# Three edits in a four-layer cross-attention kernel: order of weight splits and loads in layer 2, place of the value-bias work in layer 2, place of the second context sum in layer 3

## Chip, cores and metric

The kernel runs on one core of one Trainium2 chip. The metric is device time in microseconds (us) of one execution, lower is better. The engines are TensorE (PE; its weight loads are PEld), VectorE (DVE), ScalarE (ACT), GpSimd (POOL) and SyncE (SP), which here only issues DMAs.

## What is computed

Eight sequences of 100 tokens of 512 features pass through four layers; each sequence has a context of 361 rows. Layer 0 is a Perceiver-style attention with an MLP, layer 1 an RWKV block. The change is in layers 2 and 3. Layer 2 has two cross-attentions (numbered 1 and 2) of 16 heads of 128 features, and then an MLP; layer 3 has one cross-attention with 32 query heads and 8 key and value heads of 16 features. Cut to what matters:

```python
def _cross_attention(q_in, kv_in, wq, bq, wk, bk, wv, bv, wo, bo, bias_k, bias_v):   # layer 2, twice
    qh = (q_in @ wq + bq).reshape(b, q_len, H, K)
    kh = (kv_in @ wk + bk).reshape(b, t, H, K)
    vh = (kv_in @ wv + bv).reshape(b, t, H, K)
    kh = jnp.concatenate([kh, jnp.broadcast_to(bias_k, (b, 1, H, K))], axis=1)
    vh = jnp.concatenate([vh, jnp.broadcast_to(bias_v, (b, 1, H, K))], axis=1)
    weights = jax.nn.softmax(jnp.einsum('bqhk,bthk->bhqt', qh, kh) / scale, axis=-1)
    return jnp.einsum('bhqt,bthk->bqhk', weights, vh).reshape(b, q_len, H * K) @ wo + bo
```

## The kernel before, in words

The whole program is one launch. Each stage is a block in which the five engines run instruction lists of their own, in order, and wait for each other through semaphores; a block ends when all engines are through with it. Nothing is ordered by a planner: the order of every engine's list is written out by hand. Large fp32 products are made of three reduced-precision ones: a value is rounded to a high half (ACT) and the rest is the low half (DVE or POOL), and `product` (L71, L72, L73) multiplies high by high, high by low and low by high.

**Layer 2** (`layer2_attention`) works in four steps, `half` 0 to 3: two cross-attentions by two groups of four sequences (400 tokens). One SBUF arena (`l2_arena`) holds nearly all its buffers. A half has three phases.

- The **query phase** goes over 16 heads. For each head PE turns the key weight (`turn_keys`, L2385), makes the query (`query`, L71 to L73) and multiplies it by the turned key weight (`turn_queries`, L71 to L73 again), so that scores can be taken against the raw context. ACT rounds the weights and the query (L2607, L2616, L2621); DVE makes the low halves (`split_q_w` L2844, `split_k_w` L2849, `split_queries` L2854). In halves 0 and 2 POOL multiplies the query weight of each head by the key bias (L2345, with L2339 once per pair of heads) into one buffer, `product0`, and DVE adds it up (`reduce_w0`, L2866) before it goes on to the next head's splits. Weights of q and k come in pairs of heads (`load_qk`, L2009), two pairs of buffers.
- The **attention phase** goes over the four sequences. Their context is loaded by POOL (`load_context`, L2300 to L2309: two memsets, five DMAs), two buffers.
- The **value phase** goes again over 16 heads. For head h PE does 12 matmuls (`values`), one for the bias row (`bias_values`, L2493) and then 12 of head h-1 (`project`). ACT rounds the value weight (L2719), the four parts of `u` (L2741), the output weight (L2728) and the result (L2747); POOL makes the low half of the value weight (`split_v_w`, L2322) and of the output weight (L2372); DVE makes the low half of the result (L2943) and of `u` (L2937, four a head). DVE also does the statistics of the next half (`sum_next` L2952 at head 2, `shift_next` at head 3), and POOL the power of minus one half that they need (`invert_next`, L2327, at head 4). POOL's order from the start is: low halves of value weights 0 and 1, then for each head h first that of value weight h (from head 2 on), and then that of output weight h. SP loads value weights in pairs of heads (`load_v`, L2203) into two buffers; pair p is asked for at head 2p, before the output weight of that head (`load_o`, L2209), the bias rows (L2218) and the first column of the probabilities (L2225, L2226).

The **value bias** of both cross-attentions is prepared once, in half 0, before the first head: SP loads it (L2234, L2235) behind the first key biases (L2195, L2196), DVE takes a difference (L2987), ACT rounds it (L2757), DVE takes the rest (L2990), and SP stores six rows to DRAM (L2240) and waits for them. DVE and ACT wait for these in their lists ahead of the splits of head 0, and POOL's list begins with `load_context(0)`, which waits for the stores (`v_stored`), because the context buffer lies over the arena's value-bias rows.

**Layer 3** has a query block (`layer3_queries`) and an attention block (`layer3_attention`). The context of a sequence comes from DRAM as two halves (`load_context`, L3124) into one pair of buffers, and POOL adds them (`sum_context`, L3131) into one of two buffers `cT`, from which PE makes keys (L3152) and values (L3161) for the next sequence. POOL also spreads the queries (`spread_queries`, L3141, 12 instructions a sequence). In the attention block PE does scores (L3484), turns the probabilities (L3492) and sums (L3507, L3510) for 32 heads of each of 8 sequences; DVE stacks the low halves of the next keys (`stack_lo`, L3187) at heads 20, 22, 24 and 26. The sum of sequence 0 is done in the query block; the load and the sum of sequence 1 come at the start of the attention block, and on POOL behind the spreading of the last two pairs of sequence 0.

## Time and profile before

| | us |
|---|---|
| three timed runs, median | 3300.31 |
| three timed runs, lowest and highest | 3297.93, 3303.03 |
| the profiled execution, its own time | 3297.78 |
| its span in the profile | 3296.0 |
| mean granted TensorE clock, share of full speed | 0.962 |

The span is what the engines' records cover; 1.8 us of the profiled execution lie around it. Layer 2's attention lies between about 1110 and 2720 us of the span, layer 3 from about 2900 us to the end. In the rows further down, each line of a timeline gives start, duration, engine, line, operation, output and inputs; the bracket behind it gives how long the engine stood idle before it, and what it is taken to have waited for. "issue" there means that the profile shows no releaser. Where an instruction waits for several semaphores, the profile names the one that came last by its records, which isn't always the right one.

### The profile page before, as it was taken

The numbers are of one execution on the slowest core, as the hardware profiler recorded it, in microseconds if no ns is written. First come the engines' busy times: TensorE is split into PE (matmuls) and PEld (weight loads), VectorE is DVE, ScalarE is ACT, GpSimd is POOL, SyncE is SP. The second block draws the span as 40 slices with busy tenths as digits, with TensorE's granted clock in tenths as the row PEclk, the third lists the DMA queues.
The fourth block names the chain that finished last, engine by engine and source line by source line (L and its number), as shares of the span: only waits on it lengthen the run. The fifth ranks groups of instructions, "written<-read, shape, count | busy, mean of one in ns | idle before, by whom it ended". The sixth has DMA issues, their size and how long they took to land. (4 is left out here: it accounts for less than half of the span.)

```text
span 3296.0 us, 48341 instructions
## 1 busy us (share of the span) xinstructions
PE 3017.6 (92%) x17461; PEld 2573.6 (78%) x17461; DVE 1925.4 (58%) x3925; ACT 1498.1 (45%) x3444; POOL 893.7 (27%) x927
## 2 busy tenths in 40 slices
PE   5999989798878799999999999999999997989997
PEld 4777589484534599989999899998999996965663
DVE  2454442538953476666666776657666565137775
ACT  2544442331111254456544655446554464236773
POOL 0222310326641321133011441104101151046563
PEclk9999989899988899999999999999999997988999
DMA  4231020100001320114101241103301023021110
GB/s 127 68 99 44 27 77 1 37 27 15 0 0 39 92 92 28 43 61 129 59 28 47 81 143 45 47 28 95 120 28 55 20 85 105 1 78 40 41 43 21
DMA packets 132159, 182.79 MB, mean 55 GB/s; under 512 B 17839, under 2 KB 99740, under 8 KB 131932
## 3 DMA queue, kind: packets, MB, share of 16 engines
q1 hardware_dynamic: 119204, 143.96, 14.1%
q0 software_dynamic: 12544, 35.77, 3.5%
q8 instruction: 140, 2.29, 0.3%
q14 instruction: 87, 0.71, 0.1%
q10 hardware_dynamic: 184, 0.05, 0.0%
HBM read 165.88 MB, written 13.86 MB: 55 GB/s over the span
## 5 line engine op out<-in xcount | busy, mean ns | idle before, releaser
L71 PE MATMUL l2a<-l_arena,l_arena 128*128 128x400 f32 (+2 forms) x1856 | 642.5, 346 | 36.2 <-issue 15.8
L72 PE MATMUL l2a<-l_arena,l_arena 128*128 128x400 f32 (+2 forms) x1856 | 629.9, 339 | 0.0
L73 PE MATMUL l2a<-l_arena,l_arena 128*128 128x400 f32 (+2 forms) x1856 | 629.5, 339 | 0.0
L71 PEld LDWEIGHTS l2a<-l_arena,l_arena 128*128 128x128 f32 (+1 forms) x1856 | 349.5, 188 | 48.6 <-issue 35.5
L72 PEld LDWEIGHTS l2a<-l_arena,l_arena 128*128 128x128 f32 (+1 forms) x1856 | 350.7, 189 | 2.6
L73 PEld LDWEIGHTS l2a<-l_arena,l_arena 128*128 128x128 f32 (+1 forms) x1856 | 350.0, 189 | 2.0
L2694 ACT ACTIVATE l_arena<-l2a 121x384 fp32r<-121x384 f32 (+1 forms) x208 | 99.5, 479 | 438.3 <-PE l2a L2447 438.3
L2467 PE MATMUL l2a<-l_arena,l_arena 121*128 121x384 f32 (+1 forms) x768 | 279.6, 364 | 0.0
L2468 PE MATMUL l2a<-l_arena,l_arena 121*128 121x384 f32 (+1 forms) x768 | 263.8, 344 | 0.0
L2469 PE MATMUL l2a<-l_arena,l_arena 121*128 121x384 f32 (+1 forms) x768 | 263.8, 344 | 0.0
L2317 POOL DMA_DIRECT2D p_dram_layer<-l_arena x128 | 62.9, 497 | 653.0 <-DVE l_arena L2912 651.3
L2890 DVE TENSOR_REDUCE l_arena<-l2a 128x1 f32<-128x362 f32 (+1 forms) x208 | 110.9, 533 | 203.3 <-PE l2a L73 199.4
L3546 ACT ACTIVATE probs<-probs,neg_max 100x363 f32<-100x363 f32 x256 | 151.5, 595 | 100.4 <-DVE neg_max L3608 97.0
L2937 DVE TENSOR_TENSOR l_arena<-Qp_layer,l_arena 128x400 fp32r<-128x400 f32 x256 | 164.0, 699 | 36.2 <-ACT l_arena L2741 36.1
L3608 DVE CUSTOM_DVE_ANT_0 probs<-scores,mask 100x363 f32<-100x363 f32 x256 | 134.1, 532 | 84.5 <-PE scores L3484 78.9
L432 POOL TENSOR_SCALAR probs<-probs,inverse 100x464 f32<-100x464 f32 x128 | 83.5, 653 | 299.3 <-DVE inverse L636 299.1
L3492 PEld LDWEIGHTS turned<-ident,probs 100*121 100x121 f32 x768 | 122.3, 199 | 40.5 <-ACT probs L3546 21.7
L2468 PEld LDWEIGHTS l2a<-l_arena,l_arena 121*128 121x128 f32 x768 | 144.9, 189 | 2.3
L2469 PEld LDWEIGHTS l2a<-l_arena,l_arena 121*128 121x128 f32 x768 | 144.1, 188 | 3.0
L2467 PEld LDWEIGHTS l2a<-l_arena,l_arena 121*128 121x128 f32 x768 | 144.4, 188 | 2.4
L3492 PE MATMUL turned<-ident,probs 100*121 100x100 f32 x768 | 130.3, 281 | 17.2 <-ACT probs L3546 11.2
L2912 DVE TENSOR_TENSOR l_arena<-l2a,l_arena 121x384 fp32r<-121x384 f32 (+1 forms) x208 | 112.8, 542 | 53.3 <-ACT l_arena L2694 53.3
(444 smaller groups left out, 7016.9 us busy)
## 6 DMA issues: line engine op xcount, KB each, us to landing
l_arena<-in_L_xattn_wq_dram SPq DMA_DIRECT2D x32, 512.0 KB, 3.5
l_arena<-in_L_xattn_wk_dram SPq DMA_DIRECT2D x32, 512.0 KB, 4.7
l_arena<-in_L_xattn_wv_dram SPq DMA_DIRECT2D x32, 512.0 KB, 3.5
l_arena<-in_L_xattn_wo_dram SPq DMA_DIRECT2D x64, 256.0 KB, 2.7
l_arena<-ctxT_hi POOLq DMA_DIRECT2D x16, 724.0 KB, 4.5
l_arena<-ctxT_lo POOLq DMA_DIRECT2D x16, 724.0 KB, 6.1
l0mlp_staged<-in_L_xattn_mlp_w_dram SPq DMA_DIRECT2D x16, 512.0 KB, 4.1
l2mlp_staged<-in_L_xattn_w_fc_dram SPq DMA_DIRECT2D x16, 512.0 KB, 4.3
```

What stands on the lines that cost most here:

```text
L71: pe.matmul(out, cut_a(a.hi), cut_b(b.hi), start=start, stop=False)
L72: pe.matmul(out, cut_a(a.hi), cut_b(b.lo), start=False, stop=False)
L73: return pe.matmul(out, cut_a(a.lo), cut_b(b.hi), start=False, stop=stop)
L2467: pe.matmul(out, c_hi[s][0:T2, n, rows], probsT.hi[0:T2, n, ring], start=(n == 0), stop=False)
L2468: pe.matmul(out, c_hi[s][0:T2, n, rows], probsT.lo[0:T2, n, ring], start=False, stop=False)
L2469: mm = pe.matmul(out, c_lo[s][0:T2, n, rows], probsT.hi[0:T2, n, ring], start=False, stop=(n == NT2 - 1))
L2890: dve.tensor_reduce(neg_max[0:rows, i:i + 1], ps_s[i % 3][0:rows, 1:1 + KEYS2], AX.X, ALU.max, negate=True).then_inc(maxed, 1)
L2912: dve.tensor_tensor(probsT.lo[0:T2, :, cols], ps_t[i % 2][0:T2, 0:NT2 * P].rearrange("p (n l) -> p n l", l=P)[:, :, 0:n], probsT.hi[0:T2, ...
L2937: dve.tensor_tensor(u[h % 2].lo[:, t, :].rearrange("p (b q) -> p b q", q=L), head_columns(Qp, h)[:, t], u[h % 2].hi[:, t, :].bitcast(F32). ...
L3492: mm = pe.transpose(ps_turned[h % 2][0:T3, j * L:(j + 1) * L], probs[h % PROBS][:, j * T3:(j + 1) * T3], k.ident[0:L, 0:L])
L3546: act.activation(probs[h % PROBS][:], probs[h % PROBS][:], ACT.Exp, bias=neg_max[:, h % H3:h % H3 + 1], scale=-1.0).then_inc(exped, 1)
L3608: dve.tensor_tensor_reduce(probs[h % PROBS][:], ps_scores[h % SCORES][0:L, 0:N3], mask_add[b % 2][:], -1.0, 3e38, ALU.add, ALU.min, neg_ma ...
```

## The change

Layer 2, value phase. SP asks for the value weights of pair 2 right behind those of pairs 0 and 1, and for pair p (from 3 on) at the end of head 2p-3's steps. POOL makes the low half of value weight h+2 behind that of output weight h.

Layer 2, half 0. SP loads the value bias ahead of the first key biases. DVE takes the difference at head 1 and the rest at head 3, ACT rounds at head 2. SP stores the rows behind the loads of pair 2 of the query and key weights, without waiting; it waits for them only before the first use in the value phase. POOL loads context 0 at head 6 instead of ahead of head 0, and the wait for the stores there is gone.

Layer 3. SP loads the context of sequence 1 in the query block, as soon as sum 0 is done, and POOL adds it there, ahead of the query spreading. In the attention block, for sequences from 2 on, POOL waits before the sum also for all low halves of the last keys (`lo_stacked`).

```diff
@@ layer2_attention, SP
             for half in range(STEPS):
-                load_kb(half, 0)
-                load_kb(half, 1)
                 if half == 0:
                     for n, layer in enumerate((1, 2)):
                         sp.dma_start(v_rows[0:H2, n, 0, :], bias_v).then_inc(v_loaded, 16)
                         sp.dma_start(v_rows[0:H2, n, 1, :], ins[f"L2_xattn_bv{layer}"].rearrange("(h d) -> h d", d=DH2)
                                      ).then_inc(v_loaded, 16)
-                    sp.wait_ge(v_split, 1)
...
-                    sp.wait_ge(v_stored, 96)
+                load_kb(half, 0)
+                load_kb(half, 1)
                 for p in range(2, H2 // 2):
                     load_qk(half, p)
                     load_kb(half, p)
+                    if half == 0 and p == 2:
+                        sp.wait_ge(v_split, 1)
+                        for row, part in enumerate((v_hi, v_hi, v_lo)):
+                            for n in range(LAYERS2):
+                                sp.dma_start(vb_dram[n, row].rearrange("(h d) -> h d", d=DH2),
+                                             part[0:H2, n, :].bitcast(F32)).then_inc(v_stored, 16)
...
                 load_v(half, 1)
                 load_o(half, 1)
+                load_v(half, 2)
                 wait_p0(half + 1)
+                if half == 0:
+                    sp.wait_ge(v_stored, 96)
...
                 for h in range(2, H2):
-                    if h % 2 == 0 and h >= 4:
-                        load_v(half, h // 2)
                     load_o(half, h)
                     load_vb(half, h)
                     load_p0(half, h)
+                    if h % 2 == 1 and 3 <= (h + 3) // 2 < H2 // 2:
+                        load_v(half, (h + 3) // 2)
@@ layer2_attention, POOL
-                load_context(QUAD * half)
+                if half:
+                    load_context(QUAD * half)
                 for h in range(H2):
+                    if half == 0 and h == 6:
+                        load_context(0)
...
-                    if h >= 2:
-                        split_v_w(half, h)
                     if h == 4 and half + 1 < STEPS:
                         invert_next(half)
                     pool.wait_ge(o_w_hi, H + 1)
                     pool.tensor_tensor(Wo[h % 2].lo, staged_o[h % 2], Wo[h % 2].hi.bitcast(F32), ALU.subtract
                                        ).then_inc(o_w_lo, 1)
+                    if h + 2 < H2:
+                        split_v_w(half, h + 2)
@@ layer2_attention, ACT
-            act.wait_ge(v_diff, 1)
-            act.activation(v_hi[0:H2], v_rows[0:H2, :, 2, :], ACT.Copy).then_inc(v_rounded, 1)
...
+                    if half == 0 and h == 2:
+                        act.wait_ge(v_diff, 1)
+                        act.activation(v_hi[0:H2], v_rows[0:H2, :, 2, :], ACT.Copy).then_inc(v_rounded, 1)
@@ layer2_attention, DVE
-            dve.wait_ge(v_loaded, 64)
...
                 for h in range(H2):
+                    if half == 0 and h == 1:
+                        dve.wait_ge(v_loaded, 64)
+                        dve.tensor_tensor(v_rows[0:H2, :, 2, :], v_rows[0:H2, :, 0, :], v_rows[0:H2, :, 1, :], ALU.subtract
+                                          ).then_inc(v_diff, 1)
+                    if half == 0 and h == 3:
+                        dve.wait_ge(v_rounded, 1)
+                        dve.tensor_tensor(v_lo[0:H2], v_rows[0:H2, :, 2, :], v_hi[0:H2].bitcast(F32), ALU.subtract
+                                          ).then_inc(v_split, 1)
@@ layer3_queries
             batch.load_mask(sp, ins, 0)
+            sp.wait_ge(batch.cT_summed, 1)
+            batch.load_context(sp, k, 1)
...
             batch.sum_context(pool, 0)
             pool.wait_ge(batch.rows_ready, 1)
+            batch.sum_context(pool, 1)
@@ layer3_attention
             for b in range(1, B):
-                sp.wait_ge(batch.cT_summed, b)
-                batch.load_context(sp, k, b)
                 if b >= 2:
+                    sp.wait_ge(batch.cT_summed, b)
+                    batch.load_context(sp, k, b)
                     sp.wait_ge(shifted, H3 * (b - 1))
...
             for b in range(1, B):
+                pool.wait_ge(headed, BLOCKS * PAIRS * b)
                 if b >= 2:
                     pool.wait_ge(batch.values_done, b - 1)
-                pool.wait_ge(headed, BLOCKS * PAIRS * b)
-                batch.sum_context(pool, b)
-                if b >= 2:
+                    pool.wait_ge(batch.lo_stacked, PAIRS * b)
+                    batch.sum_context(pool, b)
                     pool.wait_ge(scored, H3 * (b - 1))
```

## Rows read from the trace of the kernel before

**Rows 1.** The page's first part: busy time, share of the span and instructions
```profile
PE 3017.6 (92%) x17461; PEld 2573.6 (78%) x17461; DVE 1925.4 (58%) x3925; ACT 1498.1 (45%) x3444; POOL 893.7 (27%) x927
```

**Rows 2.** Waits of PE, whole span: us in total, times, longest
```profile
PE l2a L71 <- issue: 15.8, 11, 2.0
```

**Rows 3.** Timeline of PE, first heads of layer 2's half 0
```profile
1123.56 0.67 PE L71 MATMUL l2a<-l_arena,l_arena 128*128 128x400 f32 x1 [3.97 <-DVE l_arena L2844]
...
1134.63 0.42 PE L71 MATMUL l2a<-l_arena,l_arena 128*128 128x400 f32 x1 [3.56 <-DVE l_arena L2844]
...
1140.62 0.60 PE L2385 MATMUL l2a<-ident,l_arena 128*128 128x128 f32 x4
...
1145.42 0.60 PE L2385 MATMUL l2a<-ident,l_arena 128*128 128x128 f32 x4
```

**Rows 4.** Timeline of DVE in the same stretch
```profile
1120.75 0.41 DVE L2987 TENSOR_TENSOR l_arena<-l_arena 16x256 f32<-16x256 f32 x1 [5.86 <-DMA l_arena<-in_L_xattn_bv_dram]
...
1131.84 0.69 DVE L2866 TENSOR_REDUCE W_layer<-l_arena 128x4 f32<-128x512 f32 x1 [7.89 <-POOL l_arena L2345]
```

**Rows 5.** Timeline of POOL in half 0's query phase
```profile
1125.79 0.52 POOL L2300 MEMSET l_arena<- 1x512 f32 x1 [13.61 <-DMA vb_layer<-l_arena]
...
1130.54 1.27 POOL L2345 TENSOR_TENSOR l_arena<-l_arena,l_arena 128x512 f32<-128x512 f32 x1
```

**Rows 6.** Windows: us, busy of PE, PEld, DVE, ACT, POOL; clock; DMA; GB/s
```profile
1123.56:1131.07 7.51, 7.51 (x28) 7.18 (x28) 0.39 (x1) 2.12 (x4) 5.18 (x9) 0.64 0.41 131
```

**Rows 7.** View of line L2196, the key-bias loads: issue to landing
```profile
DMA to landing us min/median/max: 4.0/5.0/6.0
```

**Rows 8.** Timeline of SP's queue: the six stores of the value bias
```profile
1122.09 2.63 SPq L2240 DMA_DIRECT2D vb_layer<-l_arena  x6
```

**Rows 9.** Timeline of PE, value phase of half 1
```profile
1845.33 0.34 PE L2493 MATMUL l2a<-l_arena,vb_layer 128*128 128x400 f32 x1
...
1849.88 0.42 PE L71 MATMUL l2a<-l_arena,l_arena 128*128 128x400 f32 x1 [1.99 <-issue]
...
1911.84 0.35 PE L2493 MATMUL l2a<-l_arena,vb_layer 128*128 128x400 f32 x1
...
1916.41 0.34 PE L2493 MATMUL l2a<-l_arena,vb_layer 128*128 128x400 f32 x1
```

**Rows 10.** Timeline of DVE, first heads of that value phase
```profile
1845.38 2.03 DVE L2937 TENSOR_TENSOR l_arena<-Qp_layer,l_arena 128x400 fp32r<-128x400 f32 x4 [0.38 <-ACT l_arena L2741]
...
1848.53 5.34 DVE L2937 TENSOR_TENSOR l_arena<-Qp_layer,l_arena 128x400 fp32r<-128x400 f32 x4 [0.31 <-ACT l_arena L2741]
1853.79 0.62 DVE L2943 SCALAR_TENSOR_TENSOR l_arena<-l2a,params,l_arena 128x400 fp32r<-128x400 f32 x1
...
1856.69 2.47 DVE L2952 BATCH_NORM_STATS2 l_arena<-X 100x6 f32<-100x512 f32 x4
```

**Rows 11.** Timeline of POOL there: low half of value weight 2
```profile
1848.52 1.26 POOL L2322 TENSOR_TENSOR l_arena<-l_arena,l_arena 128x512 fp32r<-128x512 f32 x1
```

**Rows 12.** Timeline of PE, layer 3, first sequence
```profile
2953.63 1.58 PE L3152 MATMUL work<-cT,Wk 128*128 128x363 f32 x2 [4.03 <-POOL cT L3131]
...
2978.36 0.53 PE L3492 MATMUL turned<-ident,probs 100*121 100x100 f32 x3 [2.00 <-DVE probsT L3615]
```

**Rows 13.** Timeline of DVE there: low half of a key stack
```profile
2974.13 3.12 DVE L3187 TENSOR_TENSOR keys<-keysT,keys_hi 32x363 fp32r<-32x363 f32 x1
```

**Rows 14.** Windows again, early attention block of layer 3
```profile
2980.00:2990.00 10.00, 10.00 (x48) 7.54 (x48) 6.29 (x23) 7.07 (x15) 7.86 (x6) 0.50 0.50 163
```

**Rows 15.** Timeline of POOL, layer 3
```profile
2940.48 0.11 POOL L3424 MEMSET ones<- 121x16 f32 x1 [7.26 <-POOLq L3207]
...
2981.75 3.10 POOL L3141 TENSOR_TENSOR q_heads<-queries_hi,head_rows 32x800 fp32r<-32x800 f32 x2 [4.89 <-PE scores L3484]
...
3024.04 3.10 POOL L3141 TENSOR_TENSOR q_heads<-queries_hi,head_rows 32x800 fp32r<-32x800 f32 x2 [19.89 <-PE scores L3484]
...
3060.99 3.10 POOL L3141 TENSOR_TENSOR q_heads<-queries_hi,head_rows 32x800 fp32r<-32x800 f32 x2 [14.55 <-PE scores L3484]
```

More of the change, by code:

```diff
@@ L2236, in _ @@
                                      ).then_inc(v_loaded, 16)
-                    sp.wait_ge(v_split, 1)
-                    for row, part in enumerate((v_hi, v_hi, v_lo)):
-                        for n in range(LAYERS2):
-                            sp.dma_start(vb_dram[n, row].rearrange("(h d) -> h d", d=DH2), part[0:H2, n, :].bitcast(F32)
-                                         ).then_inc(v_stored, 16)
-                    sp.wait_ge(v_stored, 96)
+                load_kb(half, 0)
+                load_kb(half, 1)
                 for p in range(2, H2 // 2):
@@ L2985, in _ @@
             split_q_w(0, 0)
-            dve.wait_ge(v_loaded, 64)
-            dve.tensor_tensor(v_rows[0:H2, :, 2, :], v_rows[0:H2, :, 0, :], v_rows[0:H2, :, 1, :], ALU.subtract
-                              ).then_inc(v_diff, 1)
-            dve.wait_ge(v_rounded, 1)
-            dve.tensor_tensor(v_lo[0:H2], v_rows[0:H2, :, 2, :], v_hi[0:H2].bitcast(F32), ALU.subtract).then_inc(v_split, 1)
             for half in range(STEPS):
```

## The prediction, on record before the changed kernel was run

> **What bounds the kernel now.** I read the busy shares first: TensorE (PE) is busy in 92% of the span and no other engine in more than 58% [rows 1]. So an edit pays by what it takes out of PE's stalls, and by what PE loses to a low clock after a stall; work of DVE, ACT, POOL and SP costs nothing while PE doesn't wait for it. The waits of PE come second. A group stands out whose releaser the profile doesn't know: L71 behind "issue", 15.8 us in 11 waits of at most 2.0 [rows 2]. Then the timelines of the engines, side by side, at each stall.
>
> **Start of half 0.** PE stands 3.97 us at 1123.56 and 3.56 us at 1134.63, both times for L2844, the low half of a query weight [rows 3]. DVE shows why. Ahead of the splits of head 0 it waited 5.86 us for the DMA of the value bias, and later 7.89 us for POOL's first product [rows 4]. POOL stood 13.61 us until 1125.79, because `load_context(0)` waits for the stores of the value bias; only behind its memsets and five DMAs comes the product, at 1130.54 [rows 5]. This is one chain: load, difference, rounding, rest, six stores, context, product, sum, split. The clock fell with it: granted 0.64 between 1123.56 and 1131.07 [rows 6].
>
> **Value phases.** Each head is 25 matmuls, and where nothing disturbs it its period is 4.57 us (1911.84 to 1916.41) [rows 9]. From the bias matmul of head 1 to that of head 15 half 1 takes 71.08 us. Fourteen periods are 64.0, and four heads in which PE also turns a weight of the next half add an estimated 0.35 each: 65.4. So 5.7 us are lost in this half. At head 2 the cause is visible: PE goes on at 1849.88 [rows 9], 0.10 after the low half of value weight 2 is through (1848.52 + 1.26) [rows 11], which stands on POOL behind the output weight of head 1.
>
> **Layer 3.** PE waits 4.03 us for the sum of context 1, and 2.00 at 2978.36 for DVE [rows 12], which had spent 3.12 us on a low half of keys [rows 13]. Then the clock is at 0.50, the lower level, for ten us [rows 14].
>
> **The change, part by part.** The sum is made against the profiled execution's own time, 3297.8, which is 2.5 us under the median of the runs, at their low end; the same differences are then set on the median, 3300.3.
>
> A. Value bias out of the way. DVE's 5.86 and POOL's 13.61 go, so both PE stalls go: 3.97 + 3.56 = 7.5. The clock: from 1123.56 to 1131.07 (1134.63 less its 3.56) PE takes 7.51 us for what takes 4.80 later, 2.7 lost; the 5.99 from 1134.63 to 1140.62 I set against an estimated 4.2 at full clock, 1.8 lost [rows 3, 6]. In all 12.0. What is late next: the key bias now lies behind four loads on SP and lands about 5.0 us after its issue [rows 7], then product (1.27), sum (0.69) and the splits of head 2 follow [rows 4, 5]; I get them ready within 0.2 us of PE. The two DVE operations now stand at heads 1 and 3, 0.41 each [rows 4]; one of them may show, 0.4. The stores take SP's queue for 2.63 [rows 8], so pair 3 of the weights comes some 3 us later; their cover is the pair ahead of them, two periods of 4.80, and without it 3 us would be lost once. SP's later wait for the stores, ahead of the bias rows, is for DMAs hundreds of us old: nothing. The context at head 6: two memsets at 0.52 and five DMA issues take POOL about 4 us (1125.79 to 1130.54 is 4.75 [rows 5]), against two products of 1.27 in a period of 4.80: product 7 may be late by 1 to 2 us, and DVE and ACT work about a head ahead of PE, so 0; without that cover 2. The transfers of the context meet those of the weights of pair 4, which I expect hidden as well. **A gives 11.4**, bounds 7 (the first stall back in part and the context seen) and 12.
>
> B. Value weights early. POOL makes the low half of weight h+2 behind output weight h, more than a head ahead of PE, and SP loads the pairs a head sooner. At most all of 4 x 5.7 = 22.8 goes. What stays: DVE's four parts of `u` take 2.03 alone, and took 5.34 at head 2 while POOL made weights beside them [rows 10]. POOL's two operations a head don't go away, they only come in another order. With the durations of half 1, I have left: about 1.0 at head 2 (the parts of `u` late), 1.5 at head 3, where the statistics (2.47 [rows 10]) delay the low half of the result, 0.5 at head 4 for POOL's power; 3 in each of halves 0 to 2, and 1 in half 3, which has no next statistics. 22.8 - 10 = 12.8. **B gives 13**, bounds 3 (only the wait at head 2, about 2 in two halves of the four) and 22.8. SP has more room for `load_o`, since pair 2 is asked for before the wait for the probabilities; the wait for a free buffer in `load_v` is for a low half that is now made earlier: nothing.
> Here a rule must be weighed. The row shows 5.34 - 2.03 = 3.3 us more, the length of 2.6 of POOL's 1.26 [rows 10, 11]. The Trainium skill (SBUF — State Buffer, Who interferes with whom) says that a DVE instruction with two SBUF inputs contends with a GpSimd instruction that reads SBUF, and that whoever issued first holds the shared ports for the whole instruction while the other blocks. By it B could be a loss, the third rival below; the trace agrees in size, but the steady heads at 4.57 with the same two POOL operations speak against a loss each head.
>
> C. Layer 3. The sum of context 1 moves into the query block, where POOL stood idle 7.26 us before the next block [rows 15]. With the wait for its load it delays the spreading there by about 1 us, hidden behind PE's queries; if that cover is gone, 1 us. The stall of 4.03 goes. The wait for `lo_stacked` keeps later sums off DVE's low halves; behind it on POOL stands the spreading, which waits for `scored` anyway, 19.89 and 14.55 us in later sequences [rows 15]: nothing. In sequence 0 no sum is left there, so 3.12 should fall towards the half of it or less, and the 2.00 goes. The clock: the period from 2981.75 to 3024.04 is 42.3 us, the next one 36.95 [rows 15], 5.3 lost with a clock of 0.50 [rows 14]. Without the stalls in front it may still fall; I take two thirds, 3.5. **C gives 9.5**, bounds 3 (a stall is left, clock low) and 4.0 + 2.0 + 5.3 = 11.3.
>
> Sum: 11.4 + 13 + 9.5 = 33.9. On the profiled execution 3263.9, on the median **3266.4**. With the parts erring independently this case spans some 3257 to 3275.
>
> **The rivals.**
> 1. Less than forecast: the lag of DVE in the value phases eats most of B (5 left), and layer 3's second sequence stays at the low clock (C 6). For it: 5.34, and a clock that fell to 0.50 long after the stall of 4.03. 11.4 + 5 + 6 = 22: about 3278. Chance 0.18.
> 2. More: PE never waits in the value phases and the clock holds. 12 + 22.8 + 11.3 = 46: about 3254. Against it: the statistics keep their place. 0.12.
> 3. The shared access as an exclusive lock in every head: 2.03 + 0.62 + 2 x 1.26 = 5.17 a head for DVE, 0.60 over 4.57, in 56 periods 34, less the 22.8 lost now: 11 slower in B, so 33.9 - 13 - 11 = 10 gained in all, about 3290. The rule of the Trainium skill quoted above would make this of it. 0.03.
> 4. Slower, DVE the bound of the value phases: if the new order puts POOL beside the parts of `u` in each head, they take 5.34, with the split of the result 0.62, 5.96 a head [rows 10]. That is 1.39 over 4.57, 78 in 56 periods, less 22.8: 55 lost against 21 won in A and C, about 3334. It turns slower where a head's DVE chain passes about 5.4. Against: 2.03 + 0.62 leaves 1.9 us a head, and one POOL operation needs 1.26. 0.04.
> 5. No change: each stall only changes its name (pair 3 late in A, `u` in B, `probsT` in C), or the loads aren't early because a buffer is still held. Gain under 6.6, about 3298. The three stalls have different causes, so hardly all. 0.03.
>
> **Numbers.** Forecast 0.60, the rivals 0.18, 0.12, 0.03, 0.04, 0.03. 0.2% is 6.6 us, about what a measurement of this kernel can tell from no change. Faster by more: 0.60 + 0.18 + 0.12 + 0.03 = 0.93; within: 0.03; slower: 0.04. The range 3250 to 3284 takes in cases one and two and the bounds of the terms, and leaves out rivals 3 to 5 and the tails.
>
> **What would show it.** Right: PE's stalls of 3.97 and 3.56 gone, the turn of 1140.62 some 11 us earlier; the granted clock there well over 0.64. In the value phases L71 behind "issue" under about 5 us, POOL's L2322 more than a head ahead of PE, 71.08 down to about 68. In layer 3 no wait for L3131, L3187 well under 3.12, the first `scored` period near 37. Wrong: L2937 slower in most heads and PE behind L2943 or L2741 (rivals 1, 3, 4); a new wait at heads 6 to 8 of half 0 for a split or a load; PE or POOL waiting in the query block of layer 3; a period of 42 with the stalls gone.

## The result, and the profile after

The changed kernel takes 3278.41 us (median of 5 runs, 3273.79 to 3284.71), the kernel before 3300.83 in the same comparison. The ratio is 0.9937, with a 95% interval of 0.9920 to 0.9955: 22.4 us faster by the medians. The forecast was 3266.4, which is 33.9 us faster. The profiled execution has a span of 3277.1 us against 3296.0.

The two spans, cut at the same instructions of PE, tell where the 18.9 us went. Each figure is a difference of two start times in PE's timeline.

| stretch, us | before | after | |
|---|---|---|---|
| up to layer 2's first matmul (no edit there) | 1111.30 | 1109.36 | -1.94 |
| half 0, from there to the first bias matmul | 335.23 | 331.55 | -3.68 |
| the same of halves 1 to 3 (from the last bias matmul of the half before) | 971.41 | 970.94 | -0.47 |
| value phases, first to last bias matmul, halves 0, 1, 2, 3 | 74.26, 73.46, 75.97, 70.51 | 75.73, 75.99, 75.14, 67.69 | +0.35 |
| to layer 3's first query matmul | 196.02 | 195.88 | -0.14 |
| layer 3, query block from there | 32.62 | 31.15 | -1.47 |
| layer 3, from the first score to the end | 355.22 | 343.67 | -11.55 |

So the forecast's three parts came out as 3.7 instead of 11.4 (A, the start of half 0), -0.35 instead of 13 (B, the value phases), and 13.0 instead of 9.5 (C, layer 3). Of C's 13.0 the 1.47 of the query block is not the edit's: eleven profiled executions have the second sum in that block, and in nine of them it takes 32.20 to 32.72 us, as it does before (32.62); only two have 31.15 and 31.06. That leaves 11.55. A further 2.6 of the 18.9 lie in stretches without an edit of their own.

The page's first part, which answers to [rows 1]; PE's share is the same, and DVE is 62 us busier with the same 3925 instructions:

```profile
PE 3010.9 (92%) x17461; PEld 2569.7 (78%) x17461; DVE 1987.4 (61%) x3925; ACT 1495.7 (46%) x3444; POOL 897.0 (27%) x927
```

Waits of PE in the changed kernel (us in total, times, longest; lines for other waits are left out), which answer to [rows 2]. Line numbers have moved: the splits of `u` are L2944 (L2937 before), of the result L2950 (L2943), of a query weight L2851 (L2844):

```profile
PE l2a L71 <- DVE l_arena L2944: 13.0, 13, 3.0
...
PE l2a L71 <- DVE l_arena L2851: 6.7, 3, 3.5
...
PE l2a L71 <- DVE l_arena L2950: 5.0, 3, 1.7
...
PE l2a L2391 <- DMA l_arena<-in_L_xattn_wk_dram: 4.7, 1, 4.7
```

The 15.8 us behind "issue" are gone, as forecast. In their place stand 13.0 for L2944 (2.2 before), and a new wait of 4.7 for the DMA of a key weight.

**Start of half 0.** Both stalls of [rows 3] are gone. But the turn of the key weight of head 8 (the first of pair 4), which began at 1155.76, waited, and so did the query behind it. In PE's timeline:

```profile
1155.76 1.11 PE L2391 MATMUL l2a<-ident,l_arena 128*128 128x128 f32 x4 [4.69 <-DMA l_arena<-in_L_xattn_wk_dram]
1157.64 0.67 PE L71 MATMUL l2a<-l_arena,l_arena 128*128 128x400 f32 x1 [0.77 <-DVE l_arena L2851]
```

The timeline of SP has the issue of that weight, the one of POOL the context of sequence 0 right behind it:

```profile
1140.26 1.20 SPq L2009 DMA_DIRECT2D l_arena<-in_L_xattn_wk_dram  x1
```

```profile
1140.62 0.80 POOL L2306 DMA_DIRECT2D l_arena<-ctxT_hi  x1
1141.43 0.54 POOL L2306 DMA_DIRECT2D l_arena<-ctxT_lo  x1
1141.96 1.63 POOL L2312 DMA_DIRECT2D l_arena<-in_ctx_dram  x3
```

The weight landed 15.5 us after its issue, where the key weights of pairs 2 and 3 took 4.55 and 4.75. The DMA queues show why. While the context's transfers ran (1143 to 1152), queue q0 moved 2.06 MB, nearly all of the context, and q1, which has SP's loads (this weight, and behind it the next pair), only 0.61, some 70 GB/s. From 1154 to 1157, with the context nearly through, q1 moved 0.96 MB in 3 us, some 320 GB/s (columns: packets, MB, share of 16 engines):

```profile
q0 software_dynamic: 471, 2.06, 74.4%
q1 hardware_dynamic: 616, 0.61, 27.2%
```

```profile
q1 hardware_dynamic: 984, 0.96, 105.6%
```

Behind the wait the clock was at 0.57 (windows, with the columns of [rows 6]):

```profile
1155.76:1162.00 6.24, 5.47 (x19) 5.06 (x20) 5.18 (x7) 3.20 (x7) 2.00 (x2) 0.57 0.30 96
1162.00:1172.00 10.00, 10.00 (x61) 9.93 (x60) 8.65 (x13) 5.73 (x12) 3.73 (x3) 1.00 0.38 125
```

**Value phases.** PE, half 1; 1840.19 and 1913.80 are the bias matmuls of heads 1 and 15, so the 71.08 of [rows 9] became 73.61:

```profile
1840.19 0.34 PE L2499 MATMUL l2a<-l_arena,vb_layer 128*128 128x400 f32 x1
...
1857.28 0.42 PE L71 MATMUL l2a<-l_arena,l_arena 128*128 128x400 f32 x1 [1.66 <-DVE l_arena L2950]
...
1867.48 0.50 PE L71 MATMUL l2a<-l_arena,l_arena 128*128 128x400 f32 x1 [3.04 <-DVE l_arena L2944]
...
1913.80 0.34 PE L2499 MATMUL l2a<-l_arena,vb_layer 128*128 128x400 f32 x1
```

POOL in the same stretch:

```profile
1859.64 1.04 POOL L2330 TENSOR_TENSOR l_arena<-l_arena,minus_half 100x4 f32<-100x4 f32 x1 [5.86 <-DVE l_arena L2968]
1860.67 1.28 POOL L2376 TENSOR_TENSOR l_arena<-l_arena,l_arena 128x512 fp32r<-128x512 f32 x1
...
1865.65 1.25 POOL L2376 TENSOR_TENSOR l_arena<-l_arena,l_arena 128x512 fp32r<-128x512 f32 x1
```

DVE, which answers to [rows 10]:

```profile
1840.23 5.20 DVE L2944 TENSOR_TENSOR l_arena<-Qp_layer,l_arena 128x400 fp32r<-128x400 f32 x4 [0.38 <-ACT l_arena L2747]
...
1854.14 2.46 DVE L2959 BATCH_NORM_STATS2 l_arena<-X 100x6 f32<-100x512 f32 x4
...
1860.01 8.78 DVE L2944 TENSOR_TENSOR l_arena<-Qp_layer,l_arena 128x400 fp32r<-128x400 f32 x4
```

Read them together. POOL stands 5.86 us at the power (L2330), which waits for DVE's statistics, and the low halves behind it wait too. Then it runs five of them in a row, from 1860.67 to 1866.90. Beside them DVE's four parts of `u` need 8.78 us, and PE waits 3.04. Behind that wait PE's clock is at 0.69 for 5.5 us, so this period of 9.56 is 5.0 over the undisturbed 4.57 and not only 3.04:

```profile
1867.48:1873.00 5.52, 5.52 (x22) 5.48 (x23) 4.43 (x9) 1.33 (x3) 0.14 (x1) 0.69 0.64 217
```

In half 3, where there are no statistics and no power, PE never waits after head 2 and each period is 4.57. But look at DVE there:

```profile
2682.98 4.10 DVE L2944 TENSOR_TENSOR l_arena<-Qp_layer,l_arena 128x400 fp32r<-128x400 f32 x4
2687.01 0.62 DVE L2950 SCALAR_TENSOR_TENSOR l_arena<-l2a,params,l_arena 128x400 fp32r<-128x400 f32 x1
2687.55 4.10 DVE L2944 TENSOR_TENSOR l_arena<-Qp_layer,l_arena 128x400 fp32r<-128x400 f32 x4
```

The four parts take 4.10 where they take 2.03 alone, with no idle time of DVE around them. Half 3 still runs at PE's pace, but DVE has nothing left.

**Layer 3.** The wait for L3131 and the 2.00 of [rows 12] are gone, the low half that took 3.12 [rows 13] takes 0.53, and the clock of the second sequence is 1.00 (windows of the first and the second sequence):

```profile
2933.43:2970.13 36.70, 34.55 (x205) 25.07 (x206) 28.75 (x94) 28.15 (x60) 34.26 (x21) 0.82 0.17 52
2970.13:3007.05 36.92, 34.01 (x257) 22.14 (x257) 28.78 (x99) 27.93 (x59) 21.40 (x13) 1.00 0.14 47
```

### The profile page after: what moved, and what is told of

Same layout as the page of the kernel before. It is cut to its first block and busy times, and to the rows that moved or that the text cites. A ratio compares the mean times of both kernels' runs of the same rounds, so it can differ in the third digit from the quotient of the medians.

```text
span 3277.1 us, 48347 instructions
## 1 busy us (share of the span) xinstructions
PE 3010.9 (92%) x17461; PEld 2569.7 (78%) x17461; DVE 1987.4 (61%) x3925; ACT 1495.7 (46%) x3444; POOL 897.0 (27%) x927
## 3 DMA queue, kind: packets, MB, share of 16 engines
q8 instruction: 140, 2.29, 0.3%
## 5 line engine op out<-in xcount | busy, mean ns | idle before, releaser
L2944 DVE TENSOR_TENSOR l_arena<-Qp_layer,l_arena 128x400 fp32r<-128x400 f32 x256 | 243.8, 1008 | 10.3 <-ACT l_arena L2747 9.9
L583 ACT ACTIVATE probs<-probs,neg_max 100x464 f32<-100x464 f32 x128 | 87.1, 681 | 122.5 <-DVE neg_max L669 121.7
```

The lines of the kernel that those rows point to most:

```text
L2944: dve.tensor_tensor(u[h % 2].lo[:, t, :].rearrange("p (b q) -> p b q", q=L), head_columns(Qp, h)[:, t], u[h % 2].hi[:, t, :].bitcast(F32). ...
```

## The experiments

Twelve kernels, each timed four to seven times beside the kernel before. Ratios are to the kernel before of the same comparison (medians 3299.61, 3300.36 and 3302.31), with 95% intervals. Phase lengths are from each one's profiled execution, cut as in the table above.

### Context in pieces

```diff
                     if half == 0 and h == 6:
                         load_context(0)
+                    if half == 0 and h in (8, 10, 12, 14):
+                        load_piece(0, h // 2 - 3)
```

`load_context(0)` keeps the two memsets and the first DMA, and each `load_piece` issues one of the other four.

> The changed kernel, with the five DMAs of context 0 issued at heads 6, 8, 10, 12 and 14 instead of all at head 6. Theory: in the changed kernel PE's wait of 4.69 us for a key weight at 1155.76 (and 0.77 behind it, and a half clock after it) comes from the context's transfers, which share the DMA engines with pair 4 of the weights. Then the 4.69 goes, no other wait above 1 us comes in this phase, and the kernel takes 5 to 8 us less than the changed one: 3271 to 3273. Rival: pair 4 is late because the six stores held SP's queue for 2.64 us. Then the wait stays at 4 us or more and the time stays at 3278.

Measured: 3275.15 (3269.36 to 3277.00), ratio 0.9923 (0.9910 to 0.9936). The wait for the key weight is gone, and half 0 takes 322.74 us up to its first bias matmul instead of 331.55. The mechanism is as expected; the gain in the median, 3 us, is under the 5 to 8 expected, and the intervals of the two ratios overlap. The other runs say why. Nine profiled executions have the context in one go at head 6, the changed kernel's and those of eight variants below. PE's wait in them was 4.96, 4.69, 3.76, 3.62, 2.29 and 0.75 us, and in three there was none; half 0 took 331.89 us in the worst and 322.74 in the best. The four with pieces all lie between 322.55 and 322.87. So the collision comes in some executions and not in others, and costs up to 9 us where it comes. The six stores hold SP's queue in all of them alike, so they alone don't cause it.

Could the four without a wait be luck, as the three of the nine are? The issue of that key weight on SP tells the cases apart. It took 0.82 to 1.57 us in the six executions with a wait, and the weight landed 11.5 to 15.7 us after it; in the three without, it took 0.51 to 0.70, and the weight landed after 4.8 to 5.9. With pieces it was long in two of the four as well (1.43 and 1.58), but the weight then landed after 8.8 and 8.3 us, within the 10.8 after which PE is ready for it. This is the issue in the run with pieces:

```profile
1141.80 1.43 SPq L2009 DMA_DIRECT2D l_arena<-in_L_xattn_wk_dram  x1
```

So the pieces don't avoid the meeting, they make it short enough to hide. What makes SP's issue long in one execution and not in the next was not tried.

### The power later

```diff
-                    if h == 4 and half + 1 < STEPS:
+                    if h == 6 and half + 1 < STEPS:
                         invert_next(half)
```

> The changed kernel, with POOL's power (next inverse) at head 6 of the value phase instead of head 4. Theory: at head 4 POOL waits 5.9 us for the statistics and holds five low halves back, which then run as one burst of 6.2 us; DVE's four parts of u (8.78 us at 1860.01) can't proceed beside it, and PE waits 3.04 at 1867.48. Without the hold the burst goes: the period of 9.56 (8.42, 8.72 in the other halves) at head 5 falls to 5 or 6, some 3.5 us less in each of halves 0 to 2, in all 10 us less: 3268. The wait of 1.66 for the low half of the result at head 4 stays. Rival: the parts of u are slow wherever POOL works beside them, with or without a hold; then the lost time spreads over heads 5 to 8 and the kernel takes less than 3 us less.

Measured: 3260.19 (3259.20 to 3262.16), ratio 0.9881 (0.9867 to 0.9895). The value phases are 71.01, 71.02, 71.01 and 67.67, which is 13.8 us less in sum than in the changed kernel, and the period at head 5 is 4.56 where 5 or 6 was expected. The time is 18 us under the changed kernel's, 8 more than expected; about 4 of these 18 lie outside the value phases and were not traced. The 1.66 at head 4 stays. POOL no longer stands before the power, in half 1:

```profile
1857.65 1.54 POOL L2325 TENSOR_TENSOR l_arena<-l_arena,l_arena 128x512 fp32r<-128x512 f32 x1 [1.51 <-ACT l_arena L2725]
1859.16 1.38 POOL L2330 TENSOR_TENSOR l_arena<-l_arena,minus_half 100x4 f32<-100x4 f32 x1
1860.52 1.28 POOL L2376 TENSOR_TENSOR l_arena<-l_arena,l_arena 128x512 fp32r<-128x512 f32 x1
```

Half of the rival is true: the parts of `u` are slow beside POOL here too (4.22 us at 1858.50 in half 1, 4.10 a head in half 3). Its conclusion falls: no lost time spreads over the heads behind. What costs PE is the burst, not the slowing as such.

### The statistics early

```diff
@@ DVE, end of the attention phase
                     if i == STEPS2:
                         split_u(half, 0, range(2, KT))
+                        if half + 1 < STEPS:
+                            sum_next(half)
+                            shift_next(half)
@@ DVE, value phase
-                        if h == 2:
-                            sum_next(half)
-                        if h == 3:
-                            shift_next(half)
```

> The changed kernel, with the statistics of the next half (sum and shift) moved on DVE from heads 2 and 3 to the end of the attention phase, where DVE stood idle for 4.6 us; POOL's power keeps its place at head 4. Theory: both waits of PE go, the 1.66 (the low half of the result behind 2.47 us of statistics) and the burst behind the power, since what POOL waits for is then long there. The phases of halves 0 to 2 fall from 73.3 to 66 or 67 us: 18 to 21 us less in all, 3257 to 3260. Rival: the lag of DVE comes from the order of POOL's weights alone; then the 1.66 goes but a wait for u at head 5 or 6 stays, and the gain is 5 us.

Measured: 3263.93 (3259.85 to 3265.29), ratio 0.9895 (0.9880 to 0.9909). The value phases are 69.41, 69.42, 69.41 and 67.69 us: 18.6 less in sum, as expected, and PE's waits of 1.66 and 3.04 are both gone. The time is 4 us above the range expected. The phases hold; what the median lacks was not traced to one place. The collision of half 0, absent in this profile, can come in its other executions, and its layer 3 took 347.87 us in this execution where the changed kernel's took 343.67.

### Without B

```diff
@@ SP
                 load_o(half, 1)
-                load_v(half, 2)
...
                 for h in range(2, H2):
+                    if h % 2 == 0 and h >= 4:
+                        load_v(half, h // 2)
...
-                    if h % 2 == 1 and 3 <= (h + 3) // 2 < H2 // 2:
-                        load_v(half, (h + 3) // 2)
@@ POOL
                     H = H2 * half + h
+                    if h >= 2:
+                        split_v_w(half, h)
...
-                    if h + 2 < H2:
-                        split_v_w(half, h + 2)
```

> The changed kernel with the value phases as before: loads of value weights and POOL's order undone, the parts in half 0's start and in layer 3 kept. Theory: by the value phases' own lengths the second part of the change gives nothing (73.35, 73.61, 72.75 and 65.31 us against 71.89, 71.08, 73.59 and 68.13 before, 0.3 longer in sum), so this kernel is within 3 us of the changed one, 3275 to 3281. Rival, the forecast: the part is worth 13 us, and this kernel takes 3291.

Measured: 3276.76 (3272.69 to 3284.16), ratio 0.9932 (0.9919 to 0.9945) against 0.9937. B is worth nothing in the changed kernel. The forecast's 13 us are refuted.

### B's loads alone

Of the diff just above, POOL's part alone.

> The changed kernel with POOL's order in the value phases as before (low half of value weight h ahead of output weight h); SP's early loads stay. Theory: what the second part gains and loses both come from POOL's order. The first bias periods are as before (6.8 at head 1, 6.55 at head 4), no period is over 7, and the phases are 70 to 74 us long; the odd losses of half 3 (periods of 4.8 to 5.1 in every second head) come from late loads and go, so that half 3 is near 69. The kernel is within 3 us of the changed one. Rival: the early loads alone give most of what can be had and the phases of halves 0 to 2 fall to 71 or less.

Measured: 3267.65 (3263.30 to 3273.84), ratio 0.9903 (0.9887 to 0.9918): some 11 us faster than the changed kernel. The value phases are 72.98, 71.95, 72.83 and 68.56, 8.2 less in sum. The periods at head 1 of halves 0 and 2 are 8.00 and 7.84, where none over 7 was expected. Half 3 came out as expected, since its odd losses came from the late loads, but the conclusion that was put first is wrong: B isn't two sides of POOL's order. Its loads gain (9.8 us of phase length against the kernel without B), and its order takes 8.2 of that back. DVE in half 3 of this kernel, and POOL beside it:

```profile
2659.11 2.03 DVE L2944 TENSOR_TENSOR l_arena<-Qp_layer,l_arena 128x400 fp32r<-128x400 f32 x4 [0.31 <-ACT l_arena L2747]
```

```profile
2660.96 1.34 POOL L2378 TENSOR_TENSOR l_arena<-l_arena,l_arena 128x512 fp32r<-128x512 f32 x1 [1.97 <-ACT l_arena L2734]
2662.26 1.29 POOL L2325 TENSOR_TENSOR l_arena<-l_arena,l_arena 128x512 fp32r<-128x512 f32 x1
```

With the old order POOL makes both low halves in a row, nearly all of it behind the four parts, which end at 2661.14. They take 2.03, and DVE has 1.9 us idle in each head. With the new order the same four take 4.10.

### B's order alone

Of the same diff, SP's part alone.

> The changed kernel with SP's loads of value weights as before (pair p asked for at head 2p); POOL's new order stays. Theory: POOL can make a low half two heads ahead only if the weight is there; with the late load ACT rounds it late, POOL waits for it at every even head with the output weight of the next head behind that wait, and PE waits at every second head: half 3 is longer than 67.7, by 1 us at each of six heads, some 73, and the kernel takes 5 to 15 us more than the changed one. Rival: the loads land in time anyway; then half 3 stays at 67.7 and the time is the same.

Measured: 3281.27 (3273.94 to 3285.80), ratio 0.9931 (0.9916 to 0.9946): the same as the changed kernel. Half 3 is 71.08 us (periods up to 6.45) against 67.69, so the late loads cost 3.4 us there, where 5 or 6 were expected. Halves 0 to 2 are 75.34, 73.63 and 75.25, and the whole is not the 5 to 15 us slower that was expected.

### C's sum back

```diff
@@ layer3_queries
-            sp.wait_ge(batch.cT_summed, 1)
-            batch.load_context(sp, k, 1)
...
-            batch.sum_context(pool, 1)
@@ layer3_attention
             for b in range(1, B):
+                sp.wait_ge(batch.cT_summed, b)
+                batch.load_context(sp, k, b)
                 if b >= 2:
-                    sp.wait_ge(batch.cT_summed, b)
-                    batch.load_context(sp, k, b)
...
                     pool.wait_ge(batch.lo_stacked, PAIRS * b)
-                    batch.sum_context(pool, b)
+                batch.sum_context(pool, b)
+                if b >= 2:
                     pool.wait_ge(scored, H3 * (b - 1))
```

> The changed kernel, with the load and the sum of context 1 back at the start of the attention block of layer 3; the wait for the low halves (lo_stacked) of the later sequences stays. Theory: the query-phase sum is worth what the chain there shows, the stall of 4.03 us and the low clock behind it. Then PE waits about 4 us for the sum again, the first sequence and the one behind it are 8 to 12 us longer in sum, and the kernel takes 3286 to 3290 against 3278. Rival: the clock would have fallen anyway and is no part of it; then only 4 us come back, 3282.

Measured: 3281.16 (3276.16 to 3290.32), ratio 0.9949 (0.9931 to 0.9966). The wait for the sum is back in PE's timeline:

```profile
2939.25 1.58 PE L3162 MATMUL work<-cT,Wk 128*128 128x363 f32 x2 [4.04 <-POOL cT L3141]
```

The wait for `probsT` and the low clock in the second sequence (0.95 here) are not. The first sequence takes 38.54 us, against 34.55 in the changed kernel: the 4.0 of the wait. The time is the rival's, but not its reason: the clock didn't fall far, with the stall or without. The time alone doesn't tell the two kernels apart, as their intervals overlap; the timeline does.

### C without the wait for the low halves

```diff
-                    pool.wait_ge(batch.lo_stacked, PAIRS * b)
```

> The changed kernel without POOL's wait for lo_stacked ahead of the sums of layer 3. Theory: the wait keeps the sum of context 2 (3.27 us) off DVE's last low half of keys in the first sequence. Without it that low half takes over 2.5 us again (now 0.53), PE waits 1 to 2 us for the probabilities there, and the clock of the second sequence may fall (up to 5 us): 3279 to 3285. Rival: without the sum of context 1 in the first sequence POOL comes to this sum at another time anyway, and the wait is worth nothing: 3278, with a longest low half under 2 us.

Measured: 3281.11 (3277.19 to 3282.48), ratio 0.9939 (0.9919 to 0.9959). The longest low half is 1.76 us, PE has no wait of 2 us for `probsT`, and the clock of the second sequence is 1.00. The time also lies in the range expected, but the mechanism is the rival's: by the ratios (0.9939 and 0.9937) the wait alone is worth nothing. It is close, though: the last low half of keys began 0.97 us before POOL's sum.

### Without C

Both diffs above together, so that layer 3 is as before.

> The changed kernel with layer 3 as before: sum of context 1 in the attention block, no wait for lo_stacked. Undoing either half of this part alone brought no wait of 2.00 us and no fall of the clock in the second sequence. Theory: the long low half (3.12 us) needs both, a POOL that is a sum late and no wait in front of it; with both undone it is back, PE waits about 2.0 us for probsT near the end of the first sequence, the clock of the second sequence falls to 0.8 or 0.9, and layer 3's attention block is 353 to 357 us long against 343.7 in the changed kernel; the kernel takes 3288 to 3292. Rival: the fall of the clock in the kernel before was chance; then the block is 348 long, as with the sum alone back, and the kernel takes 3282.

Measured: 3292.56 (3287.79 to 3295.76), ratio 0.9972 (0.9959 to 0.9984): 0.35% or 12 us slower than the changed kernel by the ratios, 14 by the medians. The attention block is 357.97 us long, just over the 353 to 357 expected. PE, DVE and POOL near the end of the first sequence:

```profile
2971.67 0.53 PE L3502 MATMUL turned<-ident,probs 100*121 100x100 f32 x3 [2.43 <-DVE probsT L3625]
```

```profile
2967.02 3.54 DVE L3197 TENSOR_TENSOR keys<-keysT,keys_hi 32x363 fp32r<-32x363 f32 x1
```

```profile
2966.92 3.25 POOL L3141 TENSOR_TENSOR cT<-cT_hi,cT_lo 128x1444 f32<-128x1444 f32 x1
```

DVE's instruction begins 0.10 us behind POOL's and ends 0.39 behind it: it did its own half microsecond of work when POOL was through. The clock of the second sequence is 0.77. The kernel before has the same pair, 3.12 us beside a sum that began 0.52 before it. So the dip is no chance; it needs both, a POOL that is a sum late and no wait in front of the next one. Either half of C prevents it, and the parts' gains don't add.

### Both mends together, and a third

The first version has the diffs of "Context in pieces" and "The statistics early". The second has besides:

```diff
-                if half:
+                if half % HALVES:
                     load_context(QUAD * half)
-                    if half == 0 and h == 6:
-                        load_context(0)
-                    if half == 0 and h in (8, 10, 12, 14):
-                        load_piece(0, h // 2 - 3)
+                    if half % HALVES == 0 and h == 6:
+                        load_context(QUAD * half)
+                    if half % HALVES == 0 and h in (8, 10, 12, 14):
+                        load_piece(QUAD * half, h // 2 - 3)
```

> The changed kernel with both mends together: context 0 issued in five pieces at heads 6 to 14, and the statistics of the next half at the end of the attention phase. Theory: the two are in different phases and add up. The mended value phases are 5.7 to 6.6 us shorter each in halves 0 to 2 (69.4 us against 75.1 to 76.0), and half 0's query phase is 322.7 us in every execution, where the changed kernel has 331.6 in some: 3256 to 3260. The spread of its times is smaller than that of the changed kernel's (11 us). Rival: the collision with the weights comes back with pieces at other heads; then its lowest and highest stay 8 us apart and the median is at 3263, as with the statistics alone.

> As the version with both mends, and in half 2 too the context (sequence 8 in the count of both attentions) is issued in pieces at heads 6 to 14 instead of ahead of head 0. Theory: PE's wait of 3.46 us at the start of half 2 (L2851) is the same chain as the second stall of half 0: POOL issues memsets and five DMAs before the first product. It goes, with about 1.5 us of half clock behind it: 4 to 5 us less than the version with both mends, 3252 to 3255. Rival: the wait there has another cause (the splits of the first head behind the end of half 1), and nothing changes.

Measured: the first 3255.97 (3254.38 to 3257.63), ratio 0.9869 (0.9846 to 0.9892); its spread is 3.3 us against 10.9. The second **3248.48** (3247.90 to 3250.39), ratio **0.9846** (0.9827 to 0.9866): 51.9 us faster than the kernel before and 30 faster than the changed one, by the medians. The second is 4 us faster than the range expected for it. PE's wait of 3.46 at the start of half 2 is gone; one wait for L2861 (L2851 in the changed kernel) is left, the first of half 0:

```profile
PE l2a L71 <- DVE l_arena L2861: 2.4, 1, 2.4
```

Half 2 takes 322.04 us up to its first bias matmul, against 325.71 in the first version: 3.7 of the 7.5 us between the two medians. A further 2.4 of it in the two profiles lie before layer 2, where the two kernels are the same.

### The best version without B

The second version with the diff of "Without B".

> The best version so far (contexts of halves 0 and 2 in pieces, statistics early) without the second part of the change (loads and POOL's order in the value phases as before). Theory: with the statistics out of its way the second part is worth what half 3 showed, 70.5 - 67.7 = 2.8 us a half or a little more, so this version takes 11 to 16 us more than the best one: 3260 to 3265. Rival: POOL's order hardly matters once the statistics are gone; then under 5 us more.

Measured: 3269.18 (3264.86 to 3271.21), ratio 0.9897 (0.9882 to 0.9912): 21 us slower than the best version by the medians, 17 by the ratios, at or over the upper end of the 11 to 16 expected. The value phases are 73.51, 71.83, 75.73 and 71.60 against 69.39, 69.44, 69.38 and 67.67: 16.8 in sum. B, worth nothing in the changed kernel, is worth 17 to 21 us once the statistics are out of its way.

## Why the prediction was right or wrong

The direction and the range held (3250 to 3284), and the time, 3278.41, is that of the first rival, 3278. But it isn't that rival's way: it had B reduced to 5 and C to 6, where B gave nothing, C gave its forecast or a little more, and most of A was lost in the profiled execution. That the median fell on a rival's number, and within the range, is in part luck: a term of 13 that came out as nothing was covered by the width of the range, not by an insight. Two of the prediction's own signs of being wrong came true: a new wait near heads 6 to 8 of half 0 for a load, and parts of `u` slower in most heads.

- **What bounds the kernel.** Right: each gain in the runs is a PE wait or a clock stretch that goes.
- **A, the chain through load, stores and context.** Right. Without the collision half 0 takes 322.7 instead of 335.2: 12.5 us, where the sum had 11.4 to 12.0.
- **A, the context at head 6.** The failed step: "The transfers of the context meet those of the weights of pair 4, which I expect hidden as well." They are not hidden. The bound of 7, "the context seen", was still too high: 3.7 was left in the profiled execution. I had counted POOL's time for the issues and given the transfers a sentence. A key weight that lands in 4.5 to 5 us alone took 15.5, and PE was free for it 10.8 us after its issue (1155.76 - 4.69 - 1140.26). A median over executions with and without the collision takes part of this loss. The Trainium skill (DMA: Bandwidth & Descriptors, Queues, rings and completion order) says that each DMA engine takes packets in turn from the queues it has work for. The trace agrees: both queues moved packets in the same 9 us (471 and 616).
- **B, the leftovers.** The failed step: "0.5 at head 4 for POOL's power; 3 in each of halves 0 to 2". Half 1 has 5.95 (head 1), 6.46 and 9.56 in its periods, which is 1.4 + 1.9 + 5.0 = 8.3 over 4.57, without the turns of the next half. Half 3 is as forecast, 1 left (65.31 us between heads 1 and 15). The 0.5 is given without its working, and it leaves out what the power holds back on POOL: the low halves of the next weights, which then come in one burst. The experiment with the power moved by two heads gave back 13.8 us of phase length, that with the statistics moved 18.6. A smaller slip is in the 22.8: it takes the 5.7 of half 1 for all four, where the phase lengths before, less 65.4 (64.0 in half 3), give 6.5, 5.7, 8.2 and 4.1, together 24.5.
- **B, DVE's load.** The evidence against rivals 3 and 4 was that 2.03 + 0.62 leaves 1.9 us a head. That held for the old order alone. In the new one the parts of `u` take 4.10 and DVE's list has no gap; rivals 3 (4.55 for the four) and 4 (5.34) were near in cause and size, and their loss stayed away because 4.10 + 0.62, less the 0.15 by which the records overlap, is just the period of 4.57. What an added 2.46 us of statistics does to such a list is seen at head 4.
- **B, loads and order as one.** I priced them together. With the loads early, the new order costs 8.2 us in the value phases; with the statistics gone too, loads and order together gain 16.8. No run has the early loads, the old order and the early statistics together; that wasn't tried.
- **C.** The stall of 4.03, the 2.00 and the dip all went; all of the 5.3 of the second sequence's clock, where two thirds were taken, and the clock of the first sequence rose too (0.82 against 0.77 without C). 9.5 was about right: undoing C costs 12 us by the ratios and 14 by the medians, and the intervals of the two ratios don't exclude 9.5. The wait for `lo_stacked` gets no part of it on its own.
- **The rule.** DVE's 0.53 us instruction took 3.54 beside a 3.25 us one of POOL that began 0.10 before it, and the parts of `u` double beside POOL's two. The Trainium skill (SBUF — State Buffer, Who interferes with whom) says that a DVE instruction with two SBUF inputs and a GpSimd one that reads SBUF contend, and that the one that issues later is blocked until the other is through. Both rows agree. I had weighed this rule by the steady heads of the old order, in which the two engines happen to take turns, and so gave the third and fourth rivals 0.07 together.

The 1.94 us before layer 2 and up to 4 us in layer 3 differ between executions without any edit: the ten profiles with C in place have its attention block at 343.7 to 348.0. A gain of that size can't be read from one profile.

## What to carry to other kernels

Before moving a load past others, put its transfers, not only its issue, beside the loads in flight and the slack of each of their readers; one big load in pieces cost nothing here where in one go it cost up to 9 us. Before putting an instruction with a late input into an engine's list, list what is queued behind it: the price is not its own wait but the burst that follows. And where an order was found by its sums, look at whether two engines that share a path take turns in it: the same two POOL instructions a head cost DVE nothing in one order and 2 us in the other (half 3, loads early in both).

## What the hardware showed beyond that

The four parts of `u` (2.03 us alone) took 4.10, 5.20 and 8.78 beside two, three and five of POOL's low halves, with POOL's own at 1.5 instead of 1.26 at times, so in the steady heads nearly all of the waiting is DVE's. The statistics (2.47 us beside POOL's low halves in the kernel before, 2.46 with POOL idle in the changed one), and the splits of the result (L2950, 0.62), whose first input is in PSUM, didn't stretch. The waiting goes the other way too: with the power later, POOL's low half at 1869.02, in the heads in which DVE also normalizes the next tokens (L2981), took 3.00 us. PE's clock, granted at 0.57 in the 6 us behind a stall, was at 1.00 in the ten us after.
